# Writing the expert outputs once, with x carried through the sorted rows, in place of adding them to x in DRAM

## The chip, the cores and the metric

The kernel runs on one core of one Trainium2 chip. The metric is the time of one execution on the device in microseconds, smaller being better; times are medians over several executions.

## The reference

One adaLN transformer block on x of shape (2, 1024, 128) in float32. Cut to what matters here:

```python
x = x + ga * attention(layernorm(x) * (1 + ca) + sa)
h = layernorm(x) * (1 + cb) + sb
# mixture of experts: 8 experts, a softmax over gate logits, the two best kept
for i in range(8):
    wi = dispatch[:, i:i + 1]
    hid = relu(h * wi @ w1[i] + b1[i])          # 128 -> 512
    y = hid @ w2[i] + b2[i]                     # 512 -> 128
    out = where(wi > 0, y, out)                 # the last expert of a token wins
x = x + gb * out
```

The `where` overwrites, so each token's result comes from just one expert. The kernel uses that: it sorts the tokens by that expert and computes one expert per token.

## The kernel before, in words

**Attention** (both batches, 16 head pairs in all, 8 of each batch) fills the first 745 us or so. TensorE computes scores, their maxima and the sums of values; the residual stream lives in SBUF in the tile `x_sb` (128 partitions x 16 tiles x 128 features), to which each head pair's share of the output is added on VectorE (`out_add`, L1291, and for the last pair `out_add_last`, L1305).

**Experts.** For each batch, VectorE judges the gate logits (`judge`, `choose`, L1355 to L1392), scales the normalised rows by the token's score (`scaled`, L1398) and computes to which row of a sorted list each token goes (`find_slots`, L1406 to L1423). GpSimd then scatters the rows of 8 tiles of 128 tokens into a DRAM buffer `xs_dram[b]` (`scatter`, L1064), by eight indirect DMAs per batch. A row has 132 floats, 128 features and 4 copies of the token's number. The buffer has 15 tiles of 128 slots, as each expert's part is filled up to whole tiles; it was filled at the start of the kernel with rows that hold a number beyond every token (L1582). So there are 15 tiles per batch, 30 in all; below, tile k is one of these 30, tiles 0 to 14 being batch 0, and a group g is three tiles. SyncE loads a group's rows back in their new order (`slots_in`, L1625) into one of two buffers, and for each tile the weights of its expert (`expert_data`, L1613) into a ring of six.

For tile k, TensorE transposes the rows (`slots_T`, L660), computes the hidden layer (`up_e`, L674) and the output (`down_e`, L683). The order on TensorE is up(k), transpose of k+1, down(k-1). All outputs share one PSUM bank, so down(k) waits until output k-1 was copied out. The copies of the transposed rows are ScalarE's in batch 0 (L887) and VectorE's in batch 1 (`slots_out`, L1481). The output of tiles 0 to 6 is copied by ScalarE (L891), its bias added by TensorE (L686), and GpSimd multiplies it by the gate (`scale`, L1109). From tile 7 on (T_DVE = 7) VectorE adds the bias and multiplies by the gate (`y_out`, L1487 and L1489).

**Output.** SyncE writes x after attention to `out`, one batch at a time (`base`, L1552). GpSimd then adds each tile's rows to it by an indirect DMA with `compute_op=ADD` (`place`, L1102), 30 in all, the destination rows being the token numbers that came with the sorted rows; numbers beyond the last token are skipped by the bounds check.

**Order.** Every engine runs its own list in order. GpSimd's last part is scatter(0); places 0 to 5 with their scaling; scatter(1) (T_SCAT = 6); places 6 to 29. VectorE's is the last outputs of attention, then judge(1), choose(1), scaled(1), find_slots(1), then the outputs of tiles 7 to 14, then per tile of batch 1 the copy of the next transposed rows and the output of the tile before. TensorE computes the counts that find_slots(1) needs after up(6) and down(5) (T_CN = 6, L598). SyncE issues, per group, weights of its first tile, the group's rows, weights of the other two; the weights of tile k wait until output k-6 has been copied:

```python
ge(sp, s["y_copied"], k - 2 * GS + 1)          # expert_data, GS = 3
...
nc.gpsimd.indirect_dma_start(out=out, out_offset=bass.IndirectOffsetOnAxis(ap=token[:, k:k + 1], axis=0),
                             in_=ys[k % NY], in_offset=None, bounds_check=NT * P - 1, oob_is_err=False,
                             compute_op=ALU.add).then_inc(placed[k % NY], 16)      # place, L1102
```

Of the kernel before, what the change touches and what calls it, by code (L numbers as in the profile page):

```python
# [14 lines left out]
P = 128  # L15
# [14 lines left out]
NY = 14  # L30
# [4 lines left out]
ROW = D + 4  # L35
# [13 lines left out]
def build(nc, t, out):  # L49
    ctx = ExitStack()  # L50
    with ctx:
# [34 lines left out]
        def part(size):  # L86
# [33 lines left out]
        moe = sb("moe", [P, 2 * GS + 2, D])  # L120
# [16 lines left out]
        latent_raw = [moe[:].rearrange("p a d -> p (a d)")[64:128, n * HALF:(n + 1) * HALF] for n in range(2)]  # L137
        latent_raw.append(xs_row[:].rearrange("p g t d -> p (g t d)")[64:128, 0:HALF])
# [9 lines left out]
        ys = [moe[:, n, :] for n in range(2 * GS)]  # L148
        ys += [c_all[:].rearrange("p t d -> p (t d)")[:, n * D:(n + 1) * D] for n in range(NY - 2 * GS)]
        xT = [moe[:, 2 * GS + n, :] for n in range(2)]  # L150
# [6 lines left out]
        zero = sb("zero", [P, ROW])  # L157
# [100 lines left out]
            "y_scaled": "times the gate, the first tiles (gpsimd)",  # L258
            "y_scaled_1": "from tile T_DVE on (vector)",
            "token_ids": "the tokens of a group's slots, batch 0 (gpsimd)",  # L260
            "token_ids_1": "batch 1 (vector)",
# [11 lines left out]
        group_in = [sem(f"group_in{n}") for n in range(2)]  # L273
# [3 lines left out]
        base_out = [sem(f"base_out{b}") for b in range(B)]  # L277
# [74 lines left out]
        T_FEAT, T_LOG, T_CN, T_SCAT, T_DVE = (0, 2), 3, 6, 6, 7  # L352
# [12 lines left out]
        last_banks = [(ps_m[:, 0, :], ps_x[:]), (ps_x[:], ps_m[:, 1, :])]  # L365
        logit_bank = [ps_x[:], ps_m[:, 0, :]]
# [6 lines left out]
        def _(pe):  # L373
# [280 lines left out]
            def slots_T(i, k):  # L654

                g = i // GS
                if i % GS == 0:
                    pe.wait_ge(group_in[g % 2], 16 * (k // (2 * GS) + 1))
                ge(pe, s["slots_in"], k)
                nc.tensor.transpose(ps_s[:, 2, 0:P], xs_row[:, g % 2, i % GS, 0:D], ident[:]).then_inc(s["slots_T"], 1)  # L660
# [17 lines left out]
            def down_e(i, k):  # L678

                pe.wait_ge(s["hidden"], k + 1)  # L680
                ge(pe, s["y_copied"], k)
                for c in range(4):
                    ins = nc.tensor.matmul(ps_s[:, 3, 0:D], hid[i % 2][:, c * P:(c + 1) * P],  # L683
                                           w2_all[:, expert[k], c * P:(c + 1) * P], start=(c == 0), stop=(c == 3 and k >= T_DVE))
# [1014 lines left out]
```

## Time and profile before

| | |
|---|---|
| time, median of 3 runs | 848.57 us (848.39 to 851.46) |
| the profiled execution's own time | 851.01 us |
| its span, first to last instruction | 849.1 us |
| TensorE busy | 809.6 us, 95% of the span |
| GpSimd busy | 673.7 us, 79% |
| VectorE busy | 610.0 us, 72% |
| ScalarE busy | 394.5 us, 46% |
| mean granted TensorE clock | 0.977 of full speed |
| DMA, mean over the span | 42 GB/s |

The span is the part of the execution that the trace covers. Busy shares are averages over the whole of it; the change is at work only in the last 100 us and at the very start, so the views below are of those stretches. Times in them are microseconds from the start of the span.

### The profile page before, as it was taken

The page shows a single profiled execution, that of the slowest core. Times are in us where ns is not written, and L with a number is a line of the kernel's source. Part 1 is how long each engine was busy: PE and PEld are TensorE (multiplying, and loading weights), DVE is VectorE, ACT ScalarE, POOL GpSimd, SP SyncE. Part 2 cuts the span into 40 slices and gives each one's busy share as a digit, 9 for nine tenths or more (in the row PEclk, how much of TensorE's full clock was granted, in tenths as well). Part 3 has the DMA queues.
Part 4 walks back from the last instruction along what each step waited for, and adds up shares of the span by engine and source line. Part 5 has one row for each costly group of instructions (what it writes and reads, how often), then busy time and mean ns, then how long its engine had stood idle before and what let it go on. Part 6 is the DMA issues. An engine that isn't in the chain of part 4 may idle for free.

```text
span 849.1 us, 15119 instructions
## 1 busy us (share of the span) xinstructions
PE 809.6 (95%) x5220; PEld 484.4 (57%) x5220; DVE 610.0 (72%) x1169; ACT 394.5 (46%) x637; POOL 673.7 (79%) x353
## 2 busy tenths in 40 slices
PE   4878999999999999999999999999999999999894
PEld 2535556555555555555555555555555555458894
DVE  8897777787877787878787877777777756345342
ACT  3655444444444444444444445544444444425552
POOL 3488998989999797979797989898978876225786
PEclk8979999999999999999999999999999999999998
DMA  9200010101010010101010201010101011435682
GB/s 247 47 1 13 14 26 13 28 14 26 14 19 22 14 27 2 39 2 39 2 38 2 63 1 40 1 39 2 27 1 26 1 27 16 136 114 125 168 224 37
DMA packets 84281, 36.07 MB, mean 42 GB/s; under 512 B 58736, under 2 KB 72688, under 8 KB 84144
## 3 DMA queue, kind: packets, MB, share of 16 engines
q1 hardware_dynamic: 79376, 32.98, 16.7%
q0 software_dynamic: 4832, 2.15, 1.8%
q8 instruction: 43, 0.70, 0.3%
q14 instruction: 30, 0.25, 0.1%
HBM read 29.49 MB, written 6.25 MB: 42 GB/s over the span
## 4 chain that ended last, share of the span: by engine, by line
PE 89%; DVE 4%; issue 2%; POOL 2%; DMA 1%; ACT 1%; POOLq 0%; SPq 0%
PE ps_o L486 28%; PE ps_m L449 9%; PE ps_x L437 9%; PE ps_s L470 7%; PE ps_s L472 7%; PE ps_s L474 7%; PE ps_s L476 7%; PE ps_s L537 4%; PE ps_s L495 2%; PE ps_s L674 2%; PE ps_s L683 1%; POOL out_dram L1102 1%; DVE mx L1234 1%; PE ps_m L504 1%; POOL xs_dram L1064 1%
## 5 line engine op out<-in xcount | busy, mean ns | idle before, releaser
L1028 POOL TENSOR_TENSOR big<-big,probs 128x1024 f32<-128x1024 f32 x180 | 440.3, 2446 | 69.9 <-ACT probs L778 49.9
L1234 DVE TENSOR_REDUCE mx<-ps_m 128x2 f32<-128x1024 f32 x240 | 293.9, 1225 | 109.9 <-PE ps_m L449 109.5
L778 ACT ACTIVATE probs<-ps_s 128x1024 f32<-128x1024 f32 x256 | 249.0, 1024 | 170.7 <-PE ps_s L476 170.6
L486 PE MATMUL ps_o<-probs,c_all 128*64 128x512 f32 x1024 | 247.9, 605 | 0.0
L486 PEld LDWEIGHTS ps_o<-probs,c_all 128*64 128x64 f32 x1024 | 62.1, 136 | 97.1 <-ACT probs L778 41.0
L449 PE MATMUL ps_m<-k_hi,q_hi 64*128 64x512 f32 x480 | 108.4, 444 | 2.2 <-DVE mx L1234 2.2
L470 PE MATMUL ps_s<-q_hi,k_hi 64*128 64x512 f32 x512 | 102.2, 394 | 0.0
L476 PE MATMUL ps_s<-neg_row,one_row 64*128 64x512 f32 x512 | 101.9, 390 | 0.0
L472 PE MATMUL ps_s<-q_hi,k_lo 64*128 64x512 f32 x512 | 101.7, 391 | 0.0
L474 PE MATMUL ps_s<-q_lo,k_hi 64*128 64x512 f32 x512 | 101.7, 390 | 0.0
L449 PEld LDWEIGHTS ps_m<-k_hi,q_hi 64*128 64x128 f32 x480 | 46.7, 184 | 87.4 <-issue 77.0
L1028 POOL TENSOR_TENSOR big<-probs 128x1024 f32<-128x1024 f32 x30 | 71.5, 2384 | 11.5 <-ACT probs L778 11.5
L769 ACT CAST q_hi<-ps_x 128x256 fp32r<-128x256 f32 x56 | 20.9, 373 | 90.6 <-DVE ps_x L1221 90.6
L476 PEld LDWEIGHTS ps_s<-neg_row,one_row 64*128 64x128 f32 x512 | 49.0, 185 | 10.7
L474 PEld LDWEIGHTS ps_s<-q_lo,k_hi 64*128 64x128 f32 x512 | 48.7, 185 | 10.8
L472 PEld LDWEIGHTS ps_s<-q_hi,k_lo 64*128 64x128 f32 x512 | 48.6, 185 | 10.4
L470 PEld LDWEIGHTS ps_s<-q_hi,k_hi 64*128 64x128 f32 x512 | 48.7, 186 | 9.7 <-issue 3.3
L1221 DVE TENSOR_TENSOR ps_x<-ps_x,big 128x256 f32<-128x256 f32 x112 | 48.5, 433 | 3.8
L1291 DVE TENSOR_TENSOR x_sb<-x_sb,ps_s 128x512 f32<-128x512 f32 x29 | 20.0, 689 | 41.6 <-PE ps_s L537 41.0
L1216 DVE TENSOR_TENSOR ps_x<-ps_x,big 128x256 f32<-128x256 f32 x112 | 47.3, 423 | 0.0
L1219 DVE TENSOR_TENSOR big<-ps_x,big 128x256 f32<-128x256 f32 (+1 forms) x113 | 47.1, 417 | 0.0
L769 ACT CAST k_hi<-ps_x 128x256 fp32r<-128x256 f32 x56 | 21.0, 375 | 48.5 <-DVE ps_x L1221 48.5
(305 smaller groups left out, 1024.2 us busy)
## 6 DMA issues: line engine op xcount, KB each, us to landing
big<-in_experts SPq DMA_DIRECT2D x30, 322.0 KB, 3.5
big<-rd_dram SPq DMA_DIRECT2D x60, 128.0 KB, 3.0
big<-in_wqk SPq DMA_DIRECT2D x16, 256.0 KB, 2.7
neg_row<-nm SPq DMA_DIRECT2D x256, 0.5 KB, 2.0
big<-in_expert_w SPq DMA_DIRECT2D x8, 256.0 KB, 4.2
xs_dram<-zero SPq DMA_DIRECT2D x2, 990.0 KB, 10.0
xs_row<-xs_dram SPq DMA_DIRECT2D x10, 198.0 KB, 3.4
x_sb<-in_x SPq DMA_DIRECT2D x4, 256.0 KB, 3.9
```

Source lines behind the costliest of these rows:

```text
L437: ins = nc.tensor.matmul(bank, m[:, q % 2, w, twin, :], src, start=(n == 0), stop=(n == 1))
L449: ins = nc.tensor.matmul(bank[:, h, :], q_hi[rows(h), q % 3, qt * P:(qt + 1) * P], k_hi[rows(h), q % 3, kh * HALF:(kh + 1) * HALF], start= ...
L470: nc.tensor.matmul(bank[h], k_hi[rows(h), p % 3, kc], q_hi[rows(h), p % 3, qc], start=True, stop=False)
L472: nc.tensor.matmul(bank[h], k_lo[rows(h), p % 3, kc], q_hi[rows(h), p % 3, qc], start=False, stop=False)
L474: nc.tensor.matmul(bank[h], k_hi[rows(h), p % 3, kc], q_lo[rows(h), p % 3, qc], start=False, stop=False)
L476: ins = nc.tensor.matmul(bank[h], one_row[rows(h), :], neg_row[rows(h), p % 2, qc], start=False, stop=True)
L486: ins = nc.tensor.matmul(ps_o[64 * h:64 * h + 64, :], c_all[:, (p // HP) * TB + kt, :], probs[:, st % 4, h, :], start=(kt == 0), stop=(kt ...
L778: nc.scalar.activation(probs[:, st % 4, :, :], ps_s[:, 2 * (st % 2):2 * (st % 2) + 2, :], ACT.Exp, scale=SCALE).then_inc(s["probs"], 1)
L1028: V.tensor_tensor(acc[:, buf(p, half), :, :], first, probs[:, st % 4, :, :], ALU.add).then_inc(s["added"], 1)
L1216: V.tensor_tensor(straight, straight, cos_sb[:, c], ALU.mult).then_inc(s["turned"], 1)
L1221: V.tensor_tensor(straight, straight, part, ALU.add).then_inc(s["rotated"], 1)
L1234: V.reduce_max(mx[:, :, kh, qt], max_banks(q, n), AX.X).then_inc(s["max_reduced"], 1)
```

## The change

- The residual stream `x_sb` moves into the rows that are scattered: a row now has 260 floats, 128 features, 4 copies of the token's number and 128 of x (1040 B in place of 528 B). The DRAM buffer grows with it, and the fill at the start is four DMAs in place of two.
- VectorE finishes every tile: after the bias it multiplies by the gate and adds the x that came with the sorted rows (`finish`). For tiles 0 to 5 it does so between the steps of batch 1's judging. GpSimd's scaling and its copies of the token numbers are gone; VectorE copies all token numbers.
- The indirect writes to `out` have no `compute_op` any more, and the two writes of x to `out` (`base`) are gone.
- Outputs rotate over three PSUM banks in place of one, so down(k) waits for the copy of output k-3. The buffers of finished outputs are 8 in place of 14 (NY), the buffers of sorted rows 4 groups in place of 2 (NR), two of them in `hT`.
- T_DVE is 6 in place of 7, and T_SCAT 4 in place of 6: scatter(1) comes ahead of place(4).

```diff
-NY = 14
+NY = 8
+NR = 4
-ROW = D + 4
+PAD = 4
+ROW = D + PAD + D
...
-        x_sb = sb("x_sb", [P, NT, D])
         h0_row = sb("h0", [P, NT, ROW])
         h0 = h0_row[:, :, 0:D]
+        x_sb = h0_row[:, :, D + PAD:ROW]
...
-        T_FEAT, T_LOG, T_CN, T_SCAT, T_DVE = (0, 2), 3, 6, 6, 7
+        T_FEAT, T_LOG, T_CN, T_SCAT, T_DVE = (0, 2), 3, 6, 4, 6
+        Y_BANK = [ps_s[:, 3, :], ps_o[:], ps_x[:]]
...
             def down_e(i, k):
                 pe.wait_ge(s["hidden"], k + 1)
-                ge(pe, s["y_copied"], k)
+                ge(pe, s["y_copied"], k - 2)
...
             def place(k):
-                if k < T_DVE:
-                    pool.wait_ge(s["y_scaled"], k + 1)
-                else:
-                    pool.wait_ge(s["y_scaled_1"], k - T_DVE + 1)
+                pool.wait_ge(s["token_ids"], k // GS + 1)
+                pool.wait_ge(s["finished"], k + 1)
                 nc.gpsimd.indirect_dma_start(out=out, out_offset=bass.IndirectOffsetOnAxis(ap=token[:, k:k + 1], axis=0),
-                                             in_=ys[k % NY], in_offset=None, bounds_check=NT * P - 1, oob_is_err=False,
-                                             compute_op=ALU.add).then_inc(placed[k % NY], 16)
+                                             in_=ys[k % NY], in_offset=None, bounds_check=NT * P - 1,
+                                             oob_is_err=False).then_inc(placed[k % NY], 16)
-            def scale(k):
-                pool.wait_ge(s["y_copied"], k + 1)
-                V.tensor_tensor(ys[k], ys[k], mod[:, 0, 5, :], ALU.mult).then_inc(s["y_scaled"], 1)
             scatter(0)
             inverse_root(0)
-            token_ids(0)
-            token_ids(1)
             inverse_root(1)
-            pool.wait_ge(base_out[0], 16)
             for k in range(NG * GS):
                 if k == T_SCAT:
                     scatter(1)
-                    token_ids(4)
-                if k == NA * GS:
-                    pool.wait_ge(base_out[1], 16)
-                if k < T_DVE:
-                    scale(k)
                 place(k)
...
             def y_out(i, k):                                   # vector
                 dve.wait_ge(s["y_product"], k + 1)
                 ge(dve, placed[k % NY], 16 * (k // NY))
                 y = ys[k % NY]
-                V.tensor_tensor(y, ps_s[:, 3, 0:D], b2_sb[i], ALU.add).then_inc(s["y_copied"], 1)
+                V.tensor_tensor(y, Y_BANK[k % 3][:, 0:D], b2_sb[i], ALU.add).then_inc(s["y_copied"], 1)
+                finish(k)
+            def finish(k):
                 dve.wait_ge(s["y_copied"], k + 1)
-                V.tensor_tensor(y, y, mod[:, k // (NA * GS), 5, :], ALU.mult).then_inc(s["y_scaled_1"], 1)
+                y = ys[k % NY]
+                then(V.tensor_tensor(y, y, mod[:, k // (NA * GS), 5, :], ALU.mult))
+                V.tensor_tensor(y, y, xs[k // GS % NR][:, k % GS, D + PAD:ROW], ALU.add).then_inc(s["finished"], 1)
...
+            token_ids(0)
+            token_ids(1)
+            finish(0)
+            finish(1)
+            judge(1)
+            choose(1)
+            finish(2)
+            finish(3)
+            scaled(1)
+            find_slots(1)
+            finish(4)
+            finish(5)
             for k in range(T_DVE, NA * GS):
+                if k % GS == 0:
+                    token_ids(k // GS)
                 y_out(k % (2 * GS), k)
...
             def slots_in(g, par):                              # sync
-                ge(sp, s["slots_T"], GS * (g - 1))
+                if g in (2, 3):
+                    sp.wait_ge(s["out_product"], n_part(LAST, 1))
+                ge(sp, s["finished"], GS * (g - 3))
                 sp.wait_ge(scattered, 16 * TB * (b + 1))
                 rows = xs_dram[b][n * (GS * P):(n + 1) * (GS * P), :].rearrange("(t p) d -> p t d", p=P)
-                sp.dma_start(xs_row[:, par, :, :], rows).then_inc(group_in[par], 16)
+                sp.dma_start(xs[g % NR], rows).then_inc(group_in[g % NR], 16)
...
             for b in range(B):
-                sp.dma_start(xs_dram[b].rearrange("(t p) d -> p t d", p=P),
-                             zero[:].unsqueeze(1).to_broadcast([P, NSL, ROW])).then_inc(zeros_out, 16)
+                sp.dma_start(xs_dram[b][:, 0:D + PAD].rearrange("(t p) d -> p t d", p=P),
+                             zero[:].unsqueeze(1).to_broadcast([P, NSL, D + PAD])).then_inc(zeros_out, 16)
+                sp.dma_start(xs_dram[b][:, D + PAD:ROW].rearrange("(t p) d -> p t d", p=P),
+                             zero[:, 0:D].unsqueeze(1).to_broadcast([P, NSL, D])).then_inc(zeros_out, 16)
```

## Rows read from the trace of the kernel before

**Rows 1.** Windows: busy us of each engine, granted clock, DMA share, GB/s

```profile
790.00:795.00 5.00, 5.00 (x45) 4.87 (x45) 1.52 (x6) 3.04 (x13) 3.78 (x5) 1.00 0.92 259
...
805.00:810.00 5.00, 4.40 (x24) 4.19 (x25) 0.66 (x3) 2.19 (x8) 4.09 (x4) 0.66 1.10 301
...
825.00:830.00 5.00, 5.00 (x45) 4.85 (x44) 2.29 (x8) 3.05 (x11) 4.39 (x3) 1.00 1.01 251
```

**Rows 2.** Timeline of GpSimd (start us, us, engine, line, operation): places and scatters

```profile
787.24 1.60 POOL L1102 DMA_INDIRECT out_dram<-moe,token  x1 [0.84 <-POOL moe L1109]
789.15 1.01 POOL L1064 DMA_INDIRECT xs_dram<-h,slot  x1 [0.30 <-issue]
...
800.55 1.62 POOL L1102 DMA_INDIRECT out_dram<-c_all,token  x1 [0.86 <-DVE c_all L1489]
...
843.49 1.55 POOL L1102 DMA_INDIRECT out_dram<-moe,token  x1 [0.30 <-issue]
```

**Rows 3.** Line L51, the end of the program: GpSimd's drain (ns; start us)

```profile
L51 POOLq DRAIN  x1: 9960/9960/9960, 838.9 to 838.9; - x1
```

**Rows 4.** Chain of waits from batch 1's slots to its first tile

```profile
787.69 0.18 DVE slot L1418
...
798.06 3.31 DMA xs_dram<-h,slot
...
801.46 2.81 DMA xs_row<-xs_dram
...
804.68 0.30 DVE moe L1481
```

**Rows 5.** Timelines of VectorE and ScalarE in the expert part

```profile
774.15 0.23 DVE L1355 TENSOR_TENSOR wmod_sb<-ps_m,gb_sb 128x64 f32<-128x64 f32 x1 [3.73 <-PE ps_m L590]
...
781.45 2.20 DVE L1398 TENSOR_SCALAR h<-hn,rs 128x128 f32<-128x128 f32 x8
785.20 0.17 DVE L1406 COPY cn<-ps_m 128x16 f32<-128x16 f32 x1 [1.55 <-PE ps_m L599]
...
788.47 0.17 DVE L1423 TENSOR_SCALAR eid<-tcount 128x15 int32<-128x15 f32 x1
...
837.68 0.29 DVE L1487 TENSOR_TENSOR moe<-ps_s,big 128x128 f32<-128x128 f32 x1 [1.11 <-PE ps_s L683]
838.01 0.29 DVE L1489 TENSOR_TENSOR moe<-moe,mod 128x128 f32<-128x128 f32 x1
...
787.61 0.27 ACT L891 COPY c_all<-ps_s 128x128 f32<-128x128 f32 x1
```

**Rows 6.** Timeline of TensorE: transposes of tiles 12 and 27, tile 14's output, up(16)

```profile
794.39 0.27 PE L660 MATMUL ps_s<-ident,xs_row 128*128 128x128 f32 x1
...
802.06 1.15 PE L683 MATMUL ps_s<-big,hid_sb 128*128 x8 [0.58 <-DVE c_all L1487]
...
806.84 2.07 PE L674 MATMUL ps_s<-moe,big 128*128 128x128 f32 x8 [0.38 <-DVE moe L1481]
...
829.03 0.27 PE L660 MATMUL ps_s<-ident,xs_row 128*128 128x128 f32 x1
```

**Rows 7.** Timeline of SyncE's queue: loads of groups 4 and 9, the start

```profile
14.46 4.27 SPq L1582 DMA_DIRECT2D xs_dram<-zero  x2
...
54.35 3.77 SPq L1524 DMA_DIRECT2D neg_row<-nm  x6
...
789.07 0.83 SPq L1625 DMA_DIRECT2D xs_row<-xs_dram  x1
...
823.84 0.38 SPq L1625 DMA_DIRECT2D xs_row<-xs_dram  x1
```

**Rows 8.** Loads of sorted rows (L1625), landing: all ten, then group 4's alone, group 9's

```profile
DMA to landing us min/median/max: 2.6/3.4/4.6
...
DMA to landing us min/median/max: 4.5/4.5/4.5
...
DMA to landing us min/median/max: 4.4/4.4/4.4
```

More of the change, by code:

```diff
@@ L135, in build @@
         turn_b = [h2T[:, n * HALF:(n + 1) * HALF] for n in range(2)] + [rr[:, 1, :], acc[:, 2, 1, :]]
-        latent_raw = [moe[:].rearrange("p a d -> p (a d)")[64:128, n * HALF:(n + 1) * HALF] for n in range(2)]
-        latent_raw.append(xs_row[:].rearrange("p g t d -> p (g t d)")[64:128, 0:HALF])
+        latent_raw = [xs_row[:].rearrange("p g t d -> p (g t d)")[64:128, n * HALF:(n + 1) * HALF] for n in range(3)]
         latent_raw.append(rt_sb[:].rearrange("p a d -> p (a d)")[64:128, 0:HALF])
@@ L147, in build @@
         b2_sb = [ring[:, i, F + F // P:WROW] for i in range(2 * GS)]
-        ys = [moe[:, n, :] for n in range(2 * GS)]
-        ys += [c_all[:].rearrange("p t d -> p (t d)")[:, n * D:(n + 1) * D] for n in range(NY - 2 * GS)]
-        xT = [moe[:, 2 * GS + n, :] for n in range(2)]
+        ys = [c_all[:].rearrange("p t d -> p (t d)")[:, n * D:(n + 1) * D] for n in range(NY)]
+        xT = [moe[:, n, :] for n in range(2)]
+        xs = [xs_row[:, n, :, :] for n in range(2)]
+        xs += [hT[:, n * GS * ROW:(n + 1) * GS * ROW].rearrange("p (t d) -> p t d", d=ROW) for n in range(2)]
         hid = [hid_sb[:, n, :] for n in range(2)]
@@ L257, in build @@
             "y_copied": "and in SBUF (scalar, from tile T_DVE on vector with b2)",
[L258 to L261, printed above, removed]
+            "finished": "times the gate, plus the tokens' x (vector)",
+            "token_ids": "the tokens of a group's slots (vector)",
         }
@@ L272, in build @@
         zeros_out, scattered = sem("zeros_out"), sem("scattered")
-        group_in = [sem(f"group_in{n}") for n in range(2)]
+        group_in = [sem(f"group_in{n}") for n in range(NR)]
         weights_in = sem("weights_in")
@@ L1472, in _ @@
                     recip_last(1)
-            judge(1)
-            choose(1)
-            scaled(1)
-            find_slots(1)
             def slots_out(i, k):
@@ L1547, in inv_spread @@
                                      rd_dram[half, h:h + 1, :].to_broadcast([64, HALF])).then_inc(inv_in, 16)
-            def base(b):
-                sp.wait_ge(s["out_added"], n_part(HP * (b + 1) - 1, 1))
-                sp.dma_start(out[b * S:(b + 1) * S, :].rearrange("(t p) d -> p t d", p=P),
-                             x_sb[:, b * TB:(b + 1) * TB, :]).then_inc(base_out[b], 16)
             def expert_weights(e0, e1):
@@ L1604, in _ @@
                     weights(p + 4)
-                if p == HP + 1:
-                    base(0)
             def expert_data(g, par, i):
@@ L1632, in group @@
                 expert_data(g, par, 2)
-                if g == 1:
-                    base(1)
             sp.wait_ge(s["divided"], n_part(LAST - 1, 1))
@@ L1643, in _ @@
                 sp.wait_ge(placed[n], 16 * ((NG * GS - 1 - n) // NY + 1))
-            for b in range(B):
-                sp.wait_ge(base_out[b], 16)
 def tables():
```

45 lines of the change are left out of this document (15 added, 30 removed).

## Prediction

> **What bounds the kernel now.** I read the windows first, to see which engine has no idle time in each stretch of the last 100 us; then the timeline of GpSimd and the chain of waits; then VectorE, ScalarE, TensorE and SyncE's queue at the places where these hand work to each other.
>
> The attention is TensorE's and the change does not touch it, except at the start (below). In the experts' part TensorE is busy for all of 790 to 795 and of 825 to 830 [rows 1], about 2.0 us a tile. But it does not set the end. VectorE finishes the last tile at 838.01 + 0.29 = 838.30 [rows 5], and the last place starts only at 843.49 [rows 2]. The places of tiles 6 to 29 start from 800.55 to 843.49, 24 starts with 23 steps of 1.87 us, of which 1.55 is busy and 0.30 between two [rows 2]. The reader should see that every place but the first few is released by nothing but the one before it. So the end is: scatter(1) finished, then 24 x 1.87 us of GpSimd, then the drain that starts at 838.9 and takes 9.96 us, to 848.9 [rows 3], which is 849.1 - 845.04 = 4.06 us from the end of the last place to the end of the span.
>
> The other chain starts at the same place. Batch 1's slots are there at 787.69 + 0.18 = 787.87, eight scatters follow, the last starting at 798.06 and landing 3.31 later, then the rows of group 5 take 2.81, and the first transposed rows are copied at 804.68 [rows 4]. From there TensorE needs until 838.30, about 33.6 us for 15 tiles. If GpSimd gets faster, this tile chain is late next.
>
> **Part by part.** *Plain writes in place of adding.* No plain bounded write to `out` is in this trace. The nearest rows from both sides are the scatter, an indirect DMA of as many rows without bounds check, (798.06 - 789.15) / 7 = 1.27 us from start to start, and the place itself, 1.87 [rows 2, 4]. What differs between them is the addition and the bounds check. I take 1.27, as the addition is the larger part of what an address generator must describe, and keep 1.87. The Trainium skill, "DMA: Bandwidth & Descriptors" (SDMA does more than copy), says that adding in a DMA reduces two streams; it gives no price for generating its descriptors, no row here separates them, and the sum goes by the scatter's row. With 26 places left after scatter(1) in place of 24, GpSimd's chain is 26 x 1.27 = 33 us from about 798.3: tile 29's place could start at 830, so it waits for VectorE from batch 1 on. The addition itself, one more VectorE operation of 0.29 us, 0.33 from start to start [rows 5], comes behind tile 29's gate: 838.63. Then 0.1 for the hand-over, 0.97 for the last place and 4.06 behind it: 843.8, or 5.3 us less, if the tile chain stays where it is. It does not.
>
> *GpSimd ahead of scatter(1).* Place(5) keeps GpSimd until 787.24 + 1.60 = 788.84, and the scatter starts at 789.15 though the slots are there at 787.87 [rows 2, 4]. Now only places 0 to 3 are ahead. Place(3) waits for finish(3), after choose(1), about 782.7, so GpSimd is free by 784.1. Scatter(1) then starts at 788.1, 1.0 earlier. Nothing else on GpSimd is passed, and its six scalings and token copies go with no gain of their own.
>
> *The slots themselves.* Finish(0) and (1) and two token copies, 4 x 0.33 + 0.3, lie in VectorE's 3.73 us of waiting before 774.15 [rows 5]. Finish(2) and (3) cost 1.3 us ahead of scaled(1), which now runs from 782.8 to 785.0; find_slots(1) waits for TensorE's counts until 785.20, with 1.55 us of idle ahead of it [rows 5]. So they cost nothing; if that cover were gone, they would cost the slots up to 1.3.
>
> *The stall that I expect: group 4.* Output 6 was copied by ScalarE at 787.61 + 0.27 = 787.88 [rows 5]. That releases the weights of tile 12 and, right behind them in SyncE's queue, the rows of group 4, issued at 789.07, landing 4.5 us later at 793.6, while TensorE transposes tile 12 at 794.39 [rows 6, 7, 8]. The slack is 0.8 us. Now output 6 is VectorE's, behind find_slots(1), which ends at 788.47 + 0.17 = 788.64 [rows 5], behind finish(4) and (5), 1.3, a token copy (0.17, as a small operation [rows 5]) and its own 0.29: 790.4, or 2.5 us later. Group 4 is issued at 791.6. Its load is 399 KB in place of 198 KB. The 201 KB more, at the 251 GB/s of a stretch with the DMA engines full [rows 1], are 0.8 us; so 5.3 us, landing at 796.9, and the transpose of tile 12 is 2.5 us late. The queue can be better or worse than that: ten such loads took 2.6 to 4.6 [rows 8], so I keep 2.6 + 0.8 from below (0.6 late) and twice 4.5 from above (6.2 late), the latter because the scatter's rows doubled too and pass through the same engines in 789 to 798. By the fit of 2.0 us plus bytes / 436 GB/s in the Trainium skill, "DMA: Bandwidth & Descriptors" (Anatomy of one DMA — SWDGE (gpsimd) path), such a load would take 2.5 us before and 2.9 after, and group 4 would land in time to cost about nothing; the trace has 4.5 where this fit says 2.5, and I go by the trace.
>
> From tile 12's transpose to the end of tile 14's output is 803.21 - 794.39 = 8.8 us [rows 6], so batch 0 ends at 805.7. VectorE then takes output 14 and finishes it (1.0 with the hand-over) before it copies tile 15's transposed rows: 806.8 against 804.68 [rows 4], 2.1 us late. This delay goes through to the end, as TensorE has no idle time in which to win it back.
>
> *What else meets there.* Group 5: scatter(1) starts its last at 797.0, landed at 800.3, rows in by 800.3 + 0.1 + 2.81 + 0.8 = 804.0, so before 805.7: hidden. The ring of 8 outputs: output 14 needs place(6) landed; it starts at 800.8, as third after the scatter, and with the scatter's 3.31 lands at 804.1, ahead of 805.8: hidden too, but by little; it is the cover of NY = 8. Later groups: group 9 was issued at 823.84 and took 4.4, to 828.2, with tile 27 transposed at 829.03 [rows 6, 7, 8]; 0.8 more is a tie. I add 0.4 for such small stalls: 2.5 us in all.
>
> *Costed at nothing.* Three banks: the waits on the single bank were 0.58 once in batch 0 [rows 6] and as much at the end, each also covered by ScalarE's hidden layer. One bias matmul fewer lies ahead of group 4's stall. The two writes of x to `out` were waited for by nobody, and their going helps the queue a little. The fill at the start is issued from 14.46 and moves 4 MB in place of 2, some 8 us more of DMA; the next transfers that anybody waits for are the maxima at 54.35 [rows 7], 20 us after it ends. VectorE's four operations a tile, 1.3 us, fit in TensorE's 2.0.
>
> **The sum.** -5.3 + 2.5 = -2.8 us on the span. The profiled execution itself took 851.01, so it would be 848.2; the runs' median is 848.57, 2.4 below that execution, so the median would be 845.8 us, 0.33% less. A measurement of this kernel can tell about 0.5%, 4.2 us, from no change.
>
> **The rivals.**
> 1. *The load is hidden anyway.* Group 4 lands within 3.4 to 4.5 us and is 0.6 to 1.7 late. Then batch 0 ends at 803.8 to 804.9, tile 15's rows are copied up to 1.3 after 804.68, and the time is 5.1 to 4.0 less, 844.0 in the middle. For it: base's writes and the adding are gone from the queue. Against it: the DMA engines are 0.92 busy in 790 to 795 at 259 GB/s [rows 1], before rows doubled. The fit in the Trainium skill, "DMA: Bandwidth & Descriptors" (Anatomy of one DMA — SWDGE (gpsimd) path), leads to this case.
> 2. *GpSimd stays the bound.* If the bounds check and not the addition makes the place long, it stays at 1.87, and there are two more of them behind scatter(1): 798.3 + 25 x 1.87 = 845.0, + 1.55 + 4.06 = 850.6, against 849.1: 1.5 more, 850.1. It decides from about 1.7 us a place on ((841.2 - 798.3) / 25). For it: the place takes 1.55 every time, however few of its rows are valid [rows 2], as a check per row would. Against it: an addition could be as constant.
> 3. *The scatter pays for the wider rows, and it ends slower.* If 1040 B cost GpSimd twice the 0.97 busy of 528 B, scatter(1) ends 7.7 later, group 5 arrives at 811.7, place(6) lands at 811.8 and tile 15's rows are copied 8.1 late: -5.3 + 8.1 = +2.8, 851.4; with places at 1.87 as well 858. It decides once a scatter costs 0.2 more, as group 5 has 1.7 us of slack over eight. Against it: the rows' bytes pass GpSimd by, it writes an address per row.
> 4. *A second slow stretch of TensorE.* After its waits at 803 and 805 the granted clock is 0.66 in 805 to 810 and up(16) takes 2.07 [rows 1, 6] in place of 1.1. A wait of 2.5 us at tile 12 may bring another such stretch, 1.5 us: -1.3, 847.3. I count this to my own case's range.
>
> **How the numbers follow.** My case has 0.55, rival 1 0.18, rival 2 0.19, rival 3 0.08. My case alone spans 844.0 to 849.2 by the bounds of the load and the clock. The range takes in rival 1 and rival 2 and leaves out rival 3 and the far tails: 843.4 to 850.4. Faster by over 0.5% means below 844.3: most of rival 1 (0.13) and a tail of mine (0.11): 0.24. Slower by over 0.5% means above 852.8: half of rival 3 and small tails: 0.07. Within 0.5%: 0.69.
>
> **What would show it.** In the changed profile, places on GpSimd 1.27 apart where they follow one another, and idle before each place of batch 1, released by VectorE's last addition; if they stand 1.87 apart to the end, rival 2 is right. Scatters 1.27 apart, starting by 788.2 relative to the slots. Group 4's rows issued some 2.5 us later than before, landing over 4.5 us after, and TensorE waiting for it at tile 12's transpose; no wait there, and rival 1 is right. Tile 15's rows copied about 2 us later than 804.7. The span's end about 5.1 us after the last place starts. The prediction is wrong altogether if the stretch before 760 moves by more than a few tenths, which nothing here foresees, or if the drain behind the last place is not the constant that I take it for.

## The result, and the profile after

The changed kernel takes 843.94 us (median of 8 runs, 841.68 to 844.25) against 848.57 us (8 runs, 846.34 to 852.10): a ratio of 0.9936, 95% interval 0.9917 to 0.9956. Measured once more beside other kernels, it was 0.9936 again (0.9911 to 0.9960). So it is faster by 0.4 to 0.8%, where the forecast was 845.8, a ratio of 0.9967, which is outside the interval (the time itself is at the low end of the range, 843.4 to 850.4).

The two profiled executions are further apart than the medians: 841.68 us against 851.01 (spans 839.7 and 849.1). The profiled execution of before was a long one of its kind and that of after a short one. So I read the traces from landmarks, not from the span's start. Rows of the page of the changed kernel (engine: busy us, share, instructions):

```profile
PE 807.2 (96%) x5218; PEld 481.1 (57%) x5218; DVE 616.9 (73%) x1212; ACT 394.3 (47%) x636; POOL 652.0 (78%) x341
```

GpSimd has 21.7 us less to do, VectorE 6.9 more. The landmarks are tile 0's transpose (the start of the experts' part on TensorE), the start of batch 1's counts on TensorE (L598), up(15), the end of VectorE's last operation, and the end of the span. In us, each from the one before it:

| | tile 0 | to counts | to up(15) | to VectorE's end | to the span's end | counts to end |
|---|---|---|---|---|---|---|
| before | 761.26 | 23.29 | 20.67 | 33.08 | 10.80 | 64.55 |
| after | 757.89 | 21.53 | 22.74 | 31.62 | 5.92 | 60.28 |
| difference | -3.4 | -1.8 | +2.1 | -1.5 | -4.9 | -4.3 |

The first two differences are chance (below). The last three are what the change does; how much of the -1.5 every execution has is not certain.

*The end.* The timeline of GpSimd, changed kernel, answers to [rows 2]: the last scatter, places 4, 5, 27, 28 and 29.

```profile
792.34 0.96 POOL L1065 DMA_INDIRECT xs_dram<-h,slot  x1 [0.30 <-issue]
793.61 0.99 POOL L1091 DMA_INDIRECT out_dram<-c_all,token  x1 [0.30 <-issue]
794.90 1.00 POOL L1091 DMA_INDIRECT out_dram<-c_all,token  x1 [0.30 <-issue]
...
831.27 0.98 POOL L1091 DMA_INDIRECT out_dram<-c_all,token  x1 [0.92 <-DVE c_all L1465]
833.06 0.98 POOL L1091 DMA_INDIRECT out_dram<-c_all,token  x1 [0.81 <-DVE c_all L1465]
834.64 0.98 POOL L1091 DMA_INDIRECT out_dram<-c_all,token  x1 [0.60 <-issue]
```

A place takes 0.98 us where it took 1.55, and stands 1.28 from the next where it stood 1.87. From tile 16 on GpSimd waits for VectorE. A scatter takes 0.96 us with 1040 B rows as it did with 528 B rows. The chain of waits of the same stretch shows a price that I took far too low. No place of batch 1 waited before the change, but two places in [rows 2] did, with 0.84 and 0.86 us of idle time in front of them:

```profile
830.13 0.30 DVE c_all L1465
830.43 0.02 issue
830.45 0.02 POOLq L1090
830.47 0.04 issue
830.51 0.03 POOLq L1091
830.54 0.73 issue
831.27 0.98 POOL out_dram L1091
```

From the end of VectorE's last operation on tile 27 at 830.43 to that tile's place at 831.27 are 0.84 us. The hand-over to an indirect DMA on an idle GpSimd costs that, not the 0.1 that I took.

*The middle.* TensorE, changed kernel, tile 12 and the start of batch 1; this answers to [rows 6]:

```profile
790.45 0.33 PE L660 MATMUL ps_s<-ident,xs_row 128*128 128x128 f32 x1 [1.56 <-DMA xs_row<-xs_dram]
...
791.90 1.82 PE L674 MATMUL ps_s<-moe,big 128*128 128x128 f32 x8
...
802.16 1.16 PE L674 MATMUL ps_s<-moe,big 128*128 128x128 f32 x8 [1.13 <-DVE moe L1451]
...
803.81 1.16 PE L674 MATMUL ps_s<-moe,big 128*128 128x128 f32 x8 [0.38 <-DVE moe L1451]
```

SyncE's queue, and the landing of that one load (L1606 in 786 to 787):

```profile
786.29 0.39 SPq L1606 DMA_DIRECT2D xs_row<-xs_dram  x1
...
DMA to landing us min/median/max: 4.1/4.1/4.1
```

Group 4's rows are issued 3.61 us behind the slots (VectorE's L1392, done at 782.51 + 0.17 = 782.68), where it was 1.20; they land 4.1 later, and TensorE waits 1.56 us for them at tile 12, which it did not before. Then it runs a stretch at the lower clock: up(12) takes 1.82 in place of 1.1. The windows show the clock and the DMA engines there (busy us of each engine, granted clock, DMA share, GB/s):

```profile
785.00:790.00 5.00, 3.88 (x34) 3.57 (x32) 3.07 (x12) 2.62 (x10) 3.78 (x5) 1.00 0.76 224
790.00:795.00 5.00, 4.46 (x24) 4.24 (x25) 0.88 (x3) 2.35 (x10) 3.78 (x5) 0.72 0.88 334
```

In turn, up(16) no longer takes 2.07 as in [rows 6] but 1.16: the lower clock behind tile 15 did not come in this execution. TensorE stood 1.13 us ahead of up(15) here, and 1.10 + 0.58 = 1.68 us before the change:

```profile
804.31 0.33 PE L660 MATMUL ps_s<-ident,xs_row 128*128 128x128 f32 x1 [1.10 <-DMA xs_row<-xs_dram]
805.22 1.13 PE L674 MATMUL ps_s<-moe,big 128*128 128x128 f32 x8 [0.58 <-DVE moe L1481]
```

*Batch 1.* The starts of up(17) and up(29), first in the kernel before, then in the changed kernel, split the time from up(15) to VectorE's end:

```profile
810.31 1.06 PE L674 MATMUL ps_s<-moe,big 128*128 128x128 f32 x8
833.97 1.06 PE L674 MATMUL ps_s<-moe,big 128*128 128x128 f32 x8
...
805.81 1.12 PE L674 MATMUL ps_s<-moe,big 128*128 128x128 f32 x8
829.27 1.06 PE L674 MATMUL ps_s<-moe,big 128*128 128x128 f32 x8
```

| us | up(15) to up(17) | to up(29) | to VectorE's end | sum |
|---|---|---|---|---|
| before | 5.09 | 23.66 | 4.33 | 33.08 |
| after | 3.65 | 23.46 | 4.51 | 31.62 |
| changed kernel again (below) | 3.65 | 22.82 | 4.51 | 30.98 |

So nearly all of the difference in the first pair of traces, 1.44 us, is the lower clock at up(16) and the matmuls behind it.

### The profile page after: what moved, and what is told of

It reads as the page before. It is cut to its first block, busy times and chain, and to the rows that moved or that the text cites. A ratio compares the mean times of both kernels' runs of the same rounds, so it can differ in the third digit from the quotient of the medians.

```text
span 839.7 us, 15145 instructions
## 1 busy us (share of the span) xinstructions
PE 807.2 (96%) x5218; PEld 481.1 (57%) x5218; DVE 616.9 (73%) x1212; ACT 394.3 (47%) x636; POOL 652.0 (78%) x341
## 4 chain that ended last, share of the span: by engine, by line
PE 91%; DVE 5%; DMA 1%; issue 1%; ACT 1%; POOL 0%; SPq 0%; POOLq 0%; DVEq 0%
PE ps_o L486 28%; PE ps_m L449 10%; PE ps_x L437 9%; PE ps_s L470 7%; PE ps_s L472 7%; PE ps_s L474 7%; PE ps_s L476 7%; PE ps_s L537 4%; PE ps_s L674 2%; PE ps_s L495 2%; DVE mx L1208 1%; PE ps_m L504 1%; PE ps_x L684 1%; DMA wmod_sb<-in_wmod 1%; PE ps_s L449 1%
## 5 line engine op out<-in xcount | busy, mean ns | idle before, releaser
L1091 POOL DMA_INDIRECT out_dram<-c_all,token x30 | 29.6, 985 | 29.9 <-DVE c_all L1465 21.4
L1265 DVE TENSOR_TENSOR h<-h,ps_s 128x512 f32<-128x512 f32 x29 | 20.0, 688 | 41.6 <-PE ps_s L537 41.0
```

## The experiments

All ratios are to the kernel before, with 95% intervals; a kernel's profile is one execution. Where an edit makes the kernel leave something out, the expectation says what. The theories: **A**, the addition made the places long and GpSimd was the bound, and the rest of the change costs 2 to 3 us at group 4; **B**, the gain came from the DMA queues; **C**, the tile chain is the end anyhow; the later ones stand in the expectations.

**The addition alone, taken out of the kernel before.**

```diff
-                                             in_=ys[k % NY], in_offset=None, bounds_check=NT * P - 1, oob_is_err=False,
-                                             compute_op=ALU.add).then_inc(placed[k % NY], 16)
+                                             in_=ys[k % NY], in_offset=None, bounds_check=NT * P - 1, oob_is_err=False
+                                             ).then_inc(placed[k % NY], 16)
```

> The kernel before with the addition alone taken out of its 30 indirect writes (it leaves out adding the expert output to x; the bounds check, the 24 places behind scatter(1) and all else stay). Theory A, the addition is what made a place long and GpSimd was the bound: places 1.28 us apart, GpSimd idle before the places of the last tiles, end of the span about 5.9 us behind VectorE's last multiplication, which stays about 77 us behind tile 0's transpose; time ratio to before 0.994 to 0.995 (4 to 5 us less). Theory B, the gain of the change came from the DMA queues (no read of the result, no write of x) and not from GpSimd's spacing: places stay near 1.87 and the ratio is 1.000. Theory C, the tile chain ends no later than GpSimd's anyhow: ratio above 0.998.

Measured: 841.04 us, 0.9923 (0.9897 to 0.9948). Its last places on GpSimd:

```profile
830.50 0.98 POOL L1102 DMA_INDIRECT out_dram<-c_all,token  x1 [1.02 <-DVE c_all L1488]
832.31 0.98 POOL L1102 DMA_INDIRECT out_dram<-moe,token  x1 [0.83 <-DVE moe L1488]
834.04 0.98 POOL L1102 DMA_INDIRECT out_dram<-moe,token  x1 [0.75 <-issue]
```

0.98 with the bounds check still there: the 0.57 us are the addition's. The edit of one operand in 30 DMAs gives all that the whole change gives; the ratio is even below the 0.994 to 0.995 expected, though the interval reaches into that. It was run again beside the changed kernel:

> The kernel before without the addition in its indirect writes, once more (it leaves out adding the expert output to x), beside the changed kernel on the same chip. Theory A: most of what the change brings is the addition's going, and the rest of the change gives 2 to 3 us back (batch 1's first tile comes 2 to 3 us later behind the counts, and one more step on VectorE): 0.992 here against 0.994 to 0.995 for the changed kernel. Rival: both are the same within 0.001.

Measured: 842.75 us (838.73 to 846.37), 0.9916 (0.9885 to 0.9947), against 0.9936 (0.9911 to 0.9960) for the changed kernel. The medians are on A's side, but the intervals overlap, so that the rest of the change gives anything back is not shown in the time. In the traces it is: up(15) starts 19.6 and 20.6 us behind the counts in the two profiles of this kernel, and 22.7 and 23.0 in the two of the changed kernel.

**The changed kernel with the addition put back.**

```diff
-                                             oob_is_err=False).then_inc(placed[k % NY], 16)
+                                             oob_is_err=False, compute_op=ALU.add).then_inc(placed[k % NY], 16)
```

> The changed kernel with the addition put back into its indirect writes, as the only difference (it adds to a result that nobody set, so it leaves out a defined base). Theory A: places 1.87 us apart from scatter(1) to the end, 26 of them, GpSimd is the bound again and the end is 25 x 1.87 + 1.55 + 4.1 = 52.4 us behind place(4)'s start; against the changed kernel 5 to 7 us more, so ratio to before 1.000 to 1.003. Theory B: under 2 us more than the changed kernel, ratio 0.994 to 0.996. Theory C: the VectorE part of the change gains by itself, ratio 0.997 or less although places stand 1.87 apart.

Measured: 850.32 us, 1.0016 (1.0002 to 1.0031). GpSimd is the bound to the end:

```profile
797.35 1.60 POOL L1091 DMA_INDIRECT out_dram<-c_all,token  x1 [0.30 <-issue]
...
842.10 1.61 POOL L1091 DMA_INDIRECT out_dram<-c_all,token  x1 [0.30 <-issue]
844.01 1.56 POOL L1091 DMA_INDIRECT out_dram<-c_all,token  x1 [0.30 <-issue]
```

From place(4) to place(29) are 46.7 us, 25 x 1.87, as expected. So theory A's first half holds from both sides, B and C fall. What the queues add by the addition's going, ahead of tile 15, is not separated from chance: 19.6 and 20.6 us from the counts to up(15) in b_plain's two profiles against 20.7 before. What the changed kernel would be without the cheaper place is my rival 2, 1.5 us slower; here it is, at +1.6 (850.32 against 848.67).

**Output 6 on ScalarE again.** `T_DVE = 7`, and `token_ids(2)`, `finish(6)` behind `finish(5)`.

> The changed kernel with output 6 copied by ScalarE again (T_DVE = 7, its bias by TensorE), its finishing still on VectorE behind find_slots(1). Theory A, output 6 on VectorE is what made the rows of group 4 late: group 4's rows are issued 2 to 2.5 us earlier relative to batch 1's slots, TensorE waits under 0.3 us for tile 12's rows, no stretch of low clock right behind it; 1 to 3 us less than the changed kernel, ratio to before 0.990 to 0.993. Theory D, the load was late because it is twice as large: the wait at tile 12 stays over 1 us and the ratio stays at 0.994.

Measured: 845.83 us, 0.9959 (0.9945 to 0.9973): if anything slower than the changed kernel. TensorE's wait at tile 12 fell from 1.56 to 0.53 as theory A said, and yet nothing was won. VectorE, at outputs 12 and 14, and the copy of tile 16's rows, then TensorE's up(15):

```profile
801.43 0.29 DVE L1457 TENSOR_TENSOR c_all<-ps_s,big 128x128 f32<-128x128 f32 x1 [3.06 <-DMA out_dram<-c_all,token]
...
803.73 0.29 DVE L1457 TENSOR_TENSOR c_all<-ps_x,big 128x128 f32<-128x128 f32 x1 [0.20 <-DMA out_dram<-c_all,token]
...
807.26 0.29 DVE L1451 COPY moe<-ps_s 128x128 f32<-128x128 f32 x1 [2.38 <-PE ps_s L660]
...
804.93 2.08 PE L674 MATMUL ps_s<-moe,big 128*128 128x128 f32 x8 [2.01 <-DVE moe L1451]
```

VectorE now stands 3.06 us at output 12, waiting until place(4), behind scatter(1), has landed: the ring of 8 buffers. TensorE therefore waits 2.01 us for VectorE's copy of tile 15's rows. From the counts up(15) still starts 1.1 us sooner than in the changed kernel (21.7 against 22.7), but up(15) and up(16) take 2.08 each, at the lower clock, and up(15) to up(17) takes 6.46 in place of 3.65. This is where the gain goes.

**Rows issued one weight load earlier.**

```diff
                 expert_data(g, par, 0)
-                slots_in(g, par)
+                if g % NA == 0:
+                    slots_in(g, par)
                 expert_data(g, par, 1)
                 expert_data(g, par, 2)
+                if g % NA != NA - 1:
+                    slots_in(g + 1, 1 - par)
```

> The changed kernel with each group's rows (but those of groups 0 and 5) issued one weight load earlier in SyncE's queue, ahead of the next group's first weights, so that they no longer wait for output 6 to be copied but for output 5. Theory A: the rows of group 4 are issued over 2 us earlier, no wait at tile 12 for rows; if the weights of tile 12 are then in time, 1 to 3 us less than the changed kernel, ratio 0.990 to 0.993. Rival: tile 12's weights, which still wait for output 6, land as late as the rows did, TensorE waits at up(12) instead of at the transpose, and the ratio stays within 0.993 to 0.995.

Measured: 844.45 us, 0.9954 (0.9935 to 0.9972): no gain either, but for another reason than the rival's. There is no wait at tile 12, neither for rows nor for weights. The wait is at tile 15 (TensorE, then VectorE's row at output 12):

```profile
801.55 0.47 PE L660 MATMUL ps_s<-ident,xs_row 128*128 128x128 f32 x1 [3.00 <-DMA xs_row<-xs_dram]
...
798.30 0.29 DVE L1457 TENSOR_TENSOR c_all<-ps_s,big 128x128 f32<-128x128 f32 x1 [4.03 <-DMA out_dram<-c_all,token]
```

and the last scatter took long to land, which holds the load of group 5 (chain of waits):

```profile
793.33 4.71 DMA xs_dram<-h,slot
798.12 3.38 DMA xs_row<-xs_dram
```

In [rows 4] the same two steps took 3.31 and 2.81. So three things end within some 3 us of one another ahead of tile 15: TensorE's late batch 0, the ring, and the chain of slots, scatter(1) and group 5. Taking away one uncovers the next. And the longer wait is paid twice: up(15) starts 0.8 us sooner behind the counts (22.0), but up(15) and up(16) take 2.08 each, and up(15) to up(17) 6.23.

**The same with 14 output buffers** (the six more in `probs`, which nobody reads any more).

> The changed kernel with rows issued one weight load earlier (as in a_rows) and with 14 buffers of finished outputs in place of 8. Theory E, behind the stall at group 4 lay a second one: output 12 needs place(4) landed, which waits for scatter(1), and VectorE stood 4.0 us there in a_rows: with 14 buffers that wait is gone, and batch 0 ends as in a_rows, before group 5 arrives; then group 5's arrival alone sets the start of batch 1, 41 to 42.5 us behind tile 0's transpose; expert part 80 to 82 us, ratio to before 0.991 to 0.994. Rival F: group 5's arrival (42.6 in a_rows) was the limit by itself, so the buffers bring nothing: ratio within 0.001 of a_rows' 0.9954.

Measured: 842.68 us, 0.9938 (0.9913 to 0.9962). VectorE's waits for the ring are gone; group 5 alone is waited for:

```profile
798.27 1.15 PE L685 MATMUL ps_x<-big,hid_sb 128*128 x8 [0.42 <-ACT hid_sb L882]
801.83 0.33 PE L661 MATMUL ps_s<-ident,xs_row 128*128 128x128 f32 x1 [2.41 <-DMA xs_row<-xs_dram]
```

From the counts to the end it takes 59.3 us, against 61.4 in a_rows: 0.8 less up to up(15), and 1.2 less from there to up(17). The lower clock is there too (up(15) takes 1.54 and up(16) 2.02), as the window shows:

```profile
802.50:807.50 5.00, 4.43 (x25) 4.07 (x26) 0.66 (x3) 1.77 (x7) 3.77 (x5) 0.66 0.99 318
```

The trace is for theory E; the times agree with it and do not exclude the rival.

**Narrow rows.** 132 floats are filled, scattered and loaded; the waits and orders are the changed kernel's.

```diff
-                                                 in_=h0_row[:, k, :], in_offset=None).then_inc(scattered, 16)
+                                                 in_=h0_row[:, k, 0:D + PAD], in_offset=None).then_inc(scattered, 16)
```

> The changed kernel with narrow rows: 132 floats are filled, scattered and loaded, as before, and VectorE's last addition adds what lies in SBUF (it leaves out carrying x); all orders and waits are those of the changed kernel. Theory A/G, the wider rows cost through the transfers: group 4's landing falls from 4.1 us to about 3.4, TensorE's wait at tile 12 from 1.6 to under 0.9, group 5 arrives 1 us earlier; 1 to 2.5 us less than the changed kernel, ratio 0.991 to 0.993. Rival: only the order of VectorE's work made group 4 late, the width costs nothing: ratio 0.994 to 0.9955. Scatters 1.27 us apart in both.

Measured: 844.40 us, 0.9945 (0.9925 to 0.9966), no different from the changed kernel. Group 4's load, issued at 788.23, landed after 3.3 us in place of 4.1, and the wait at tile 12 is 0.66 in place of 1.56:

```profile
DMA to landing us min/median/max: 3.3/3.3/3.3
...
791.59 0.33 PE L660 MATMUL ps_s<-ident,xs_row 128*128 128x128 f32 x1 [0.66 <-DMA xs_row<-xs_dram]
...
803.50 2.07 PE L674 MATMUL ps_s<-moe,big 128*128 128x128 f32 x8 [2.88 <-DVE moe L1453]
```

So the 201 KB more cost about the 0.8 us that I had worked out (4.1 and 4.3 in the two profiles of the changed kernel, 3.3 here), and the order of VectorE's work the rest. But VectorE then waits for the ring (2.43 us at output 13) and up(15) waits 2.88. It still starts 0.8 us sooner behind the counts (22.0), and then up(15) to up(17) takes 6.07 at the lower clock: the gain is lost there. Both halves of the expectation came true in the trace and neither in the time.

**One bank's wait.** `ge(pe, s["y_copied"], k - 2)` becomes `ge(pe, s["y_copied"], k)`.

> The changed kernel with the wait of the single PSUM bank: down(k) waits for the copy of output k-1 though the banks still rotate. My prediction costed the three banks at nothing; but as output 6, 7 and 8 are now copied late by VectorE, down(7), (8) and (9) would wait with one bank. Theory H: down(7) waits for output 6's copy, TensorE stands 2 to 3 us before tile 8's hidden layer is done, and all behind it is late: 1 to 3 us more than the changed kernel, ratio 0.995 to 0.998. Rival, as predicted: nothing, ratio within 0.001 of 0.9936 to 0.9945.

Measured: 844.09 us, 0.9947 (0.9926 to 0.9967). TensorE, down(7):

```profile
786.34 1.15 PE L684 MATMUL ps_o<-big,hid_sb 128*128 x8 [1.85 <-DVE c_all L1457]
```

The wait is there, 1.85 us, which I had costed at nothing; the time is within what can be told of the changed kernel's. In its one profile the counts are 62.6 us from the end against 60.3, but that execution has the lower clock behind tile 15 too. One part is free of that. From up(17) to up(29), at the full clock, this run takes 23.61 us (its rows below), as the one-bank kernels do: 23.66 before, 23.65 and, with one longer step, 24.18 in b_plain's two profiles. With three banks six profiles take 22.75 to 22.82; the other four have a longer step among these tiles and take 23.3 to 23.9.

```profile
809.28 1.09 PE L674 MATMUL ps_s<-moe,big 128*128 128x128 f32 x8
...
832.89 1.06 PE L674 MATMUL ps_s<-moe,big 128*128 128x128 f32 x8
```

So by the traces three banks are worth 0.8 us in batch 1. In the time their worth stays open between 0 and 2 us.

**Four edits together.** Rows earlier, 14 buffers, a group's rows in two loads, and tile 15's rows copied ahead of output 14.

```diff
-                sp.dma_start(xs[g % NR], rows).then_inc(group_in[g % NR], 16)
+                sp.dma_start(xs[g % NR][:, :, 0:D + PAD], rows[:, :, 0:D + PAD]).then_inc(group_in[g % NR], 16)
+                sp.dma_start(xs[g % NR][:, :, D + PAD:ROW], rows[:, :, D + PAD:ROW]).then_inc(x_rows_in[g % NR], 16)
```

> The changed kernel with four edits: rows one weight load earlier, 14 output buffers, the rows of a group in two loads (132 floats first, x behind it, waited for by VectorE alone), and tile 15's transposed rows copied ahead of output 14. Theories A and E: nothing late at tile 12, group 5's first part lands in about 3 us, up(15) starts 41.5 to 42.5 us behind tile 0's transpose (44.3 in the changed kernel, 44.0 before), end 1.5 to 3 us earlier than the changed kernel: ratio 0.990 to 0.992. Rival: the smaller pieces and one more load per group cost the queue what they save, ratio 0.994 or more.

Measured: 843.78 us, 0.9940 (0.9920 to 0.9961): the rival, by its number. In the profile it is 58.7 us from counts to end, 1.6 less than the changed kernel, but in this execution the counts come 23.15 us behind tile 0 and not 21.5, and tile 15 waits 1.88 us for group 5. Group 5's first part landed in 2.8 us: what is late is the scatter ahead of it.

**The changed kernel again.**

> The changed kernel itself, unchanged, beside the others of this call on the same chip. It tells how large the ratio is when measured again (0.9936 first) and which parts of its profile are chance: by theory A the time from TensorE's counts to the end of the span is 60 us within 1 us, or 61.5 with a stretch of the lower clock behind tile 16; the time of tile 0's transpose (757.9 in the first profile, 757.8 to 761.5 in all so far) and of the counts (21.5 or 23.1 behind it) may come out otherwise.

Measured: 843.82 us, 0.9936 (0.9911 to 0.9960). Tile 0 at 760.64 (757.89 in the first profile), 21.5 to the counts, 59.9 from there to the end; tile 12 waits 1.73. So the first 3.4 us between the two traces are chance, and the part behind the counts comes back within 0.4.

**Slots sooner.** a_best, with the chain into batch 1 started earlier:

```diff
-        T_FEAT, T_LOG, T_CN, T_SCAT, T_DVE = (0, 2), 3, 6, 4, 6
+        T_FEAT, T_LOG, T_CN, T_SCAT, T_DVE = (0, 2), 3, 5, 2, 6
...
             choose(1)
-            finish(2)
-            finish(3)
             scaled(1)
             find_slots(1)
+            finish(2)
+            finish(3)
```

> The kernel a_best with batch 1's slots found sooner: the counts one tile earlier on TensorE (T_CN = 5), scaled(1) and find_slots(1) ahead of finish(2) and (3), scatter(1) ahead of place(2) (T_SCAT = 2). Theory I, with the stall at group 4 and the ring gone the chain slots, scatter(1), group 5's rows sets the end: slots 23.2 to 23.8 us behind tile 0's transpose in place of 24.6 to 25.9, tile 15's transpose at 40.5 to 41.5, end 1 to 2.5 us before a_best's: ratio 0.990 to 0.993. Rival: output 6 and the weights of tile 12 are later still, TensorE waits there, and nothing is won: ratio 0.994 or more.

Measured: 840.26 us (838.44 to 844.22), 0.9893 (0.9873 to 0.9914). This is the shortest of all. It is clear of the kernel before and of a_best's 0.9940; the changed kernel beside it took 843.82, 0.9936 (0.9911 to 0.9960), and these intervals just touch. The slots come 23.5 us behind tile 0's transpose, group 5's rows are issued 38.0 behind it (40.0 in a_best), and nothing waits for a load any more in batch 0 or at tile 15. The profiled execution is the longest of its six runs, 844.22. Its TensorE ran up(7) in 2.08 us at the lower clock, behind a wait of 0.72 us for what VectorE hands to the counts:

```profile
785.45 2.08 PE L676 MATMUL ps_s<-moe,big 128*128 128x128 f32 x8
```

**The same order with the ring of 8 and whole rows.**

> The changed kernel with the earlier slots of a_best2 alone (T_CN = 5, T_SCAT = 2, scaled(1) and find_slots(1) ahead of finish(2)), and still 8 output buffers, whole rows in one load, issued late. Theory E, the ring of 8 is a limit as soon as scatter(1) stands ahead of more places: output 10 waits for place(2), the first behind scatter(1), so VectorE stands 3 to 6 us at output 10 and tile 15's transpose comes 43 us or later behind tile 0's though the slots come at 23.5: no gain or a loss against the changed kernel, ratio 0.993 to 0.998. Rival: the earlier slots are worth their 1.2 us whatever the ring: ratio 0.990 to 0.992.

Measured: 846.07 us, 0.9972 (0.9949 to 0.9995): no gain, and by the medians a loss against the changed kernel's 0.9936 (the intervals overlap a little), by an edit that gives the slots 1.1 us sooner. Output 10 waits for place(2), now behind scatter(1), as VectorE's row shows:

```profile
800.84 0.29 DVE L1457 TENSOR_TENSOR c_all<-ps_o,big 128x128 f32<-128x128 f32 x1 [3.39 <-DMA out_dram<-c_all,token]
```

Theory E's forecast holds: 3.39 us at output 10, tile 15's transpose 43.7 us behind tile 0's. That it is the buffers alone which the earlier order needs is not shown, as a_best2 also issues its rows earlier, in two loads, and copies tile 15's rows sooner. And part of the loss is not the ring's: as in a_best2's profile, a wait of 0.72 us at the counts is followed by up(7) in 2.08 us.

## Why the prediction was wrong

The sign was right and the size too small: -2.8 us forecast, -4.6 in the medians, -4.3 from the counts to the end in the two traces. By its steps:

- *What bounds the kernel* and *the plain write*: right. I took 1.27 us a place between 1.27 and 1.87, and it is 1.28. The trace puts the price of the addition at 0.57 us of GpSimd's time for 128 rows. The Trainium skill, "DMA: Bandwidth & Descriptors" (SDMA does more than copy), says only that adding reduces two streams. Rival 2 is out by b_plain, rival 3 by scatters of 0.96 us with the wide rows.
- *The end*: 5.3 less forecast, and 4.55 came, as the hand-over was missed: 0.84 us in place of 0.1, though [rows 2] had shown it. GpSimd's last place starts 0.86 behind VectorE's end, and the span ends 5.06 behind that start, where I had 0.97 + 4.06 = 5.03; the drain is the constant that I took it for. From VectorE's end to the span's end 5.92 in place of 10.80: 4.9, less 0.33 for VectorE's additional step.
- *VectorE's additional step*: 0.33 from start to start, right; it is inside the 31.62.
- *Slots at no cost*: right as to the waits. GpSimd was free in time, the scatter started 0.78 us behind the slots' end (the hand-over again) where it had been 1.28 behind, so 0.5 and not 1.0 was won.
- *Group 4*: issued 3.61 behind the slots against 1.20 before, 2.4 later, where 2.5 was forecast. It landed after 4.1, not 5.3. The 0.8 for the bytes is about right (a_narrow: 3.3); the start of the range, 4.5, was one load's row, and 3.3 is what a load of the old size took in its place. The fit in the Trainium skill, "DMA: Bandwidth & Descriptors" (Anatomy of one DMA — SWDGE (gpsimd) path), gives an estimate of 2.9 for this load, though it is made for GpSimd's DMAs and this is SyncE's; the trace says 4.1, between it and mine. TensorE waited 1.56 there, not 2.5, and then lost about as much again at the lower clock, my item 4. The sum by either way is close: up(15) came 2.07 later behind the counts, against 2.1 forecast. That agreement is partly luck, as two errors cancel in it.
- *The step that failed* is the next one: "This delay goes through to the end", and with it the three banks costed at nothing and the lower clock counted only as a further loss. I had 0.4 more for small stalls behind tile 15. From up(15) to VectorE's end the changed kernel takes 31.62 against 33.08, 1.5 less in place of 0.7 more (0.4 and VectorE's 0.33).
  - 1.44 of it is the lower clock at up(16) and behind it, under a granted clock of 0.66 ([rows 1, 6]), a stretch that I took as given for both. It is not. The late group 4 made batch 0 end 2.8 us later behind the counts and tile 15 only 2.1, so the delay took up a part of the time that TensorE stood ahead of tile 15 anyway, 1.68 us before and 1.13 after. Ten of the 14 profiles have up(15) or up(16) at the lower clock, and in these TensorE had stood 1.31 to 4.67 us ahead of up(15) and its transpose; in the four without it 0.38 to 1.13, the two profiles of the changed kernel among them. That is what 14 single executions show, and no run varies this wait alone, so the cause is argued and not shown.
  - 0.8 is the three banks: one tile of batch 1 follows another more closely, as a_onebank shows. In the first profile of the changed kernel a longer step from tile 26 to tile 27, the first of group 9, takes 0.6 of that back, in the second none does; my 0.4 for small stalls lies between.

  So the right working has -4.9 + 2.1 - 1.5 = -4.3, and the medians' -4.6 allows all of it. That there is less of the lower clock is not the chance of one profile: the mean granted clock was 0.981 to 0.986 in the changed kernel's eight executions, 0.985 in the median, and 0.978 to 0.984 in 25 of the kernel before, 0.980 in the median. Where in these executions the difference lies is not known.
- *Costed at nothing*: besides batch 1, the three banks spare 1.85 us of waiting at down(7). The ring of 8 was named as cover "but by little", and the runs show that it is the next wall: VectorE stands at it for 3 to 4 us in a_tdve7, a_rows and a_early8.
- *Rival 1*, with 844.0 and a chance of 0.18, has the right time, and its condition came true by its numbers: group 4 landed after 4.1 us (3.4 to 4.5) and TensorE waited 1.56 (0.6 to 1.7). But its way is not what happened: it had tile 15 at most 1.3 us late, and it was 2.1 late, with the difference won back behind it. The sign "no wait there, and rival 1 is right" did not fit the rival's own 0.6 to 1.7.
- *The sign of being wrong altogether*, a stretch before 760 that moves by more than a few tenths, came (3.4 us) and meant nothing: the same kernel's own two profiles differ there by 2.8.

The two errors in the size go opposite ways: the hand-over takes 0.75 from the gain, and the part behind tile 15 gives 2.2 to it. The forecast of "within 0.5%" with 0.69 leaned on 2.5 us of losses, of which 2.1 came, without asking which losses of the kernel before would go. "TensorE has no idle time in which to win it back" was true of its idle time behind tile 15, and not of its clock nor of the step from tile to tile.

## What to carry to other kernels

When a serial engine paces the tail, price each operand of its instructions: one operand (the addition in an indirect write) was worth the whole gain here, and what the rest of a change gives back shows only beside a kernel that has that one edit. Where several chains end within 2 us of each other, removing one stall gives nothing in the time, and a longer wait at the next can cost more than itself, by a stretch of the lower clock behind it; look in the trace for what is waited for next, and remove them together (a_best2, 1.1%, of edits that brought nothing or a loss one at a time). Compare traces from landmarks near the change, not from the start of the span.

## What the runs showed of the hardware that was not expected

- An indirect write of 128 rows costs GpSimd 1.55 us with an addition and 0.98 without, in nearly every place, though 896 of a batch's 1920 rows hold no token; a scatter costs 0.96 for rows of 528 B and of 1040 B alike.
- An indirect DMA on an idle GpSimd starts 0.78 to 0.86 us behind the event that it waited for; one behind another starts 0.30 after its end.
- TensorE's matmuls behind a wait ran at the lower clock in ten of 14 profiles at tiles 15 and 16 (granted clock 0.66 over 5 us in a_rows14): 3.65 us from up(15) to up(17) without it, 5.0 to 6.5 with it.
- Fourteen executions, whose attention on TensorE is the same program, had tile 0's transpose anywhere from 757.75 to 762.20 us. Of the twelve with the counts behind up(6), seven had them 21.5 to 21.7 us behind that, and five 23.1 to 23.3; in those five, matmuls at tiles 4 and 5 ran at the lower clock. One profile each can be 6 us apart without any cause in the code.
- The last scatter landed 3.31 us from its start in the kernel before and 4.71 in a_rows, where wider rows and more loads ran beside it.
